# Moving the first-round transposes of an attention head pair past the next pair's first scores, in a decoder layer on one core

## The chip, the cores and the metric

The kernel runs on 1 core of one Trainium2 chip. The metric is the device time of one execution in microseconds (us), as the median of several runs. Engines are named as the profile names them: PE is TensorE (PEld its weight loads), DVE is VectorE, ACT is ScalarE, POOL is GpSimd, SP is SyncE.

## The reference

A pre-norm decoder layer on x (2 batches, 512 tokens, 128 channels): causal self-attention, differential cross-attention over 154 context tokens, and a quantised feed-forward with a depthwise convolution. Only the self-attention matters here:

```python
q = jnp.einsum('ntc,hdc->nhtd', x_q, w_q)          # 16 heads of 64
k = jnp.einsum('ntc,hdc->nhtd', x_q, w_k)
v = jnp.einsum('ntc,hdc->nhtd', x_q, w_v)
a = jnp.einsum('nhtd,nhsd->nhts', q, k) / math.sqrt(q.shape[3])
a = jnp.where(causal_forbidden[None, None], -jnp.inf, a)
a = jax.nn.softmax(a, axis=3)
y = jnp.einsum('nhts,nhsd->nthd', a, v).reshape(a.shape[0], t, -1)
return y @ w_o
```

## The kernel before

The self-attention is a software pipeline over 16 steps (STEPS: 2 batches of 8 head pairs). Step n treats both heads of one pair. Its 512 query rows are four tiles of 128 rows; because of the causal mask tile t has 128(t+1) key columns. They are taken in three rounds, `ROUNDS = [[3], [2, 0], [1]]`: round 0 is tile 3 (512 columns), round 1 tiles 2 and 0 (384 and 128), round 2 tile 1 (256), each for both heads. I call round 0 the first, round 1 the second and round 2 the short round.

A round passes through all engines. `scores(n, r)` on PE writes the scores to two PSUM banks; round k = 3n + r uses pair k % 2 of two such pairs (ST0 and its neighbour, SM and its neighbour), so scores(n, 2) must wait until the exponentials of round (n, 0) have read theirs (`exp_done`), and scores(n+1, 0) for those of round (n, 1). `row_max(n, r)` on DVE reduces them (L1122 for round 0, one instruction a head; L1128 for the others). `exps(n, r)` on ACT (L414) writes the exponentials and their sums. `invert_sums` on DVE (L1136) takes reciprocals, `normalise` on POOL (L299) multiplies with them. `turn(n, r)` on PE (L677) transposes the probabilities into PSUM, 64 by 64: rounds 0 and 1 into the same two banks PT and PT + 1 (16 transposes each), round 2 into PJ0 and OB (8 transposes). The turned blocks are copied to SBUF: `keep_turned(n, 0)` on DVE (128x512, L1150) and `keep_half(n)` on ACT (L423) share those of round 0, `keep_turned(n, 1)` on DVE copies those of round 1 (128x1024, also L1150), `keep_short(n)` on ACT those of round 2 (L435). Because rounds 0 and 1 share banks, turn(n, 1) waits until both copies of round 0 are done. `weighted(n)` on PE multiplies with the values, `copy_heads` on ACT (L445) takes the result.

`project(n+1, 1)` and `project(n+1, 0)` on PE make the keys and queries of the next pair. `keys(n+1)` on DVE (L1108) and `query(n+1)` on ACT (L393) copy them to `qs`. The query projection uses bank PT, so it waits for keep_turned(n-1, 1), and scores(n+1, 0) waits for query(n+1). On ACT `query(n+1)` stands behind `exps(n, 1)`.

Each engine works through its instructions strictly in the order written; the engines meet only through semaphores. `t_ps` counts finished turns, `pt_dve` and `pt_act` finished copies. Before the change the orders of step n are:

- PE: scores(n, 0), turn(n-1, 1), scores(n, 1), turn(n-1, 2), scores(n, 2), both projections of n+1, weighted(n-1), turn(n, 0).
- DVE: keep_turned(n-1, 0), row_max(n, 0), keep_turned(n-1, 1), invert_sums(n, 0), row_max(n, 1), row_max(n, 2), keys(n+1), extras of some steps, invert_sums(n, 1), invert_sums(n, 2), extras.
- ACT: copy_heads(n-2), keep_half(n-1), exps(n, 0), keep_short(n-1), exps(n, 1), query(n+1), exps(n, 2).

Some steps carry extras: DVE quantises the two feed-forward weights behind steps 2 and 3 (`quantise_weights`), takes norm statistics behind step 10 and applies the norm behind step 11; ACT takes a square root behind step 10, which swaps its function table twice; PE does the output projection of batch 0 in step 9 behind the projections (`out_proj`, waits for keys(10)) and four 128x128 transposes in step 12 (`turn_norm`, waits for keys(13)). After step 15 cross-attention rounds (`cross_max`, `cross_row_max`) follow, interleaved with the remaining turns of the last pair.

Of the kernel before, what the change touches and what calls it, by code (L numbers as in the profile page):

```python
# [18 lines left out]
STEPS = B * NPAIR  # L19
# [45 lines left out]
def decoder_layer(nc, x, consts, wqk, wv, wo, ctxT, xwq, xbq, xwk, xbk, xwv, xbv, xwo, xbo, lam_in,  # L65
                  w1, cw, cb, w2, out):
    with ExitStack() as ctx:
# [135 lines left out]
        def sem_names(*names):  # L203
            return [sem(n) for n in names]
# [10 lines left out]
        t_ps, pt_dve, pt_act, u_ps, u_done = sem_names("t_ps", "pt_dve", "pt_act", "u_ps", "u_done")  # L215
# [150 lines left out]
        def _(act):  # L366
# [38 lines left out]
            def exps(n, r):  # L405
                k = 3 * n + r
                if n >= 1:
                    act.wait_ge(t_ps, k - 2)
                at = 0
                for t in ROUNDS[r]:  # L410
                    w = P * (t + 1)
                    for a in range(2):
                        act.wait_ge(max_done, MAXES[k] + 1 + a if r == 0 else MAXES[k + 1])
                        nc.scalar.activation(prob[r][:, a, at:at + w], bank[:, SP[k % 2] + a, at:at + w], ACT.Exp,  # L414
                                             bias=nmax[:, t, a:a + 1], accum_out=psum[:, t, a:a + 1]).then_inc(exp_done, 1)
                    at += w
# [8 lines left out]

            def keep_short(n):

                act.wait_ge(t_ps, 3 * n + 3)
                if n >= 1:
                    act.wait_ge(u_ps, n)  # L430
                for half, at in enumerate((PJ0, OB)):
                    whole = pT[:, 2, :, :]
                    dst = bass.AP(whole.tensor, whole.offset + 64 * half,
                                  [list(whole.ap[0]), [T, 2], [P, 2], [1, 64]])
                    last = nc.scalar.copy(dst, bank[:, at, 0:2 * P].rearrange("p (a i q) -> p a i q", a=2, i=2))  # L435
                last.then_inc(pt_act, 1)
# [165 lines left out]
        def _(pe):  # L602
            def mm(out_, lhsT, rhs, start, stop, **kw):
                return nc.tensor.matmul(out_, lhsT, rhs, start=start, stop=stop, **kw)  # L604
# [21 lines left out]
            def scores(n, r):  # L626

                k = 3 * n + r
                if r == 0:
                    pe.wait_ge(q_done, n + 1)  # L630
                    pe.wait_ge(k_done, n + 1)
                if k >= 2:
                    pe.wait_ge(exp_done, EXPS[k - 1])
                at = 0
                for t in ROUNDS[r]:
                    w = P * (t + 1)
                    for a in range(2):
                        own = slice(64 * a, 64 * a + 64)
                        mm(bank[:, SP[k % 2] + a, at:at + w], qs[own, 0, t * P:t * P + P], qs[own, 1, 0:w], at == 0,
                           False, skip_group_check=True)  # L640
                    at += w
                    for half in range(2):
                        for a in range(2):
                            own = slice(64 * a, 64 * a + 64)
                            last = mm(bank[:, SP[k % 2] + a, at - P:at], sel_b[own, half, :], mask_b[own, half, :], False,
                                      half == 1, skip_group_check=True)
                last.then_inc(s_ps, 1)

            def turn(n, r):

                k, blocks = 3 * n + r, (NT, NT, 2)[r]
                pe.wait_ge(norm_done, EXPS[k + 1])
                if r == 0 and n >= 1:
                    pe.wait_ge(pt_dve, 2 * n)
                if r == 0 and n + 1 < STEPS:
                    pe.wait_ge(q_done, n + 2)
                if r == 1:
                    pe.wait_ge(pt_dve, 2 * n + 1)
                    pe.wait_ge(pt_act, 2 * n + 1)
                if r == 2:  # L660
                    if n + 1 < STEPS:
                        pe.wait_ge(k_done, n + 2)
                    else:
                        pe.wait_ge(xq_act, 2)
                    if n >= 1:
                        pe.wait_ge(u_done, n)
                    if n == 9:
                        pe.wait_ge(y_done, 1)
                    if n == 12:
                        pe.wait_ge(xTl_done, 3)  # L670
                lower, upper = (PJ0, OB) if r == 2 else (PT, PT + 1)
                for a in range(2):
                    for i in range(blocks):
                        at = 64 * (blocks * a + i)
                        for half, to in enumerate((lower, upper)):
                            own = slice(64 * half, 64 * half + 64)
                            last = nc.tensor.transpose(bank[:, to, at:at + 64], prob[r][own, a, P * i:P * i + P],  # L677
                                                       con[own, C_ID + 64 * half:C_ID + 64 * half + 64])
                last.then_inc(t_ps, 1)
# [54 lines left out]
            def next_round():  # L734
                r = rounds[0]
                rounds[0] += 1
                if r >= 1:

                    pe.wait_ge(round_done, r if r < SINGLE else r - 1)
                return _round_bank(r)  # L740
# [8 lines left out]
            def cross_max(G, r):  # L749
                b, g, t, half = G // NG, G % NG, r // 2, r % 2  # L750
                if r == 0:
                    pe.wait_ge(qb0_done, G + 1)
                    pe.wait_ge(km_done, 2 * G + 2)
                at = next_round()
                for k in range(2):
                    last = mm(bank[:, at + k, 0:2 * S2],
                              qb0[:, G % 2, t * P:t * P + P],
                              km[:, g, 4 * half + 2 * k:4 * half + 2 * k + 2, :], True, True)
                last.then_inc(round_ps, 1)
# [173 lines left out]
            project(1, 1)  # L933
            pe.wait_ge(wsum_done, 1)
            project(1, 0)
            turn(0, 0)
            pe.wait_ge(vx_done, 4)

            for n in range(1, STEPS):
                scores(n, 0)  # L940
                turn(n - 1, 1)
                scores(n, 1)
                turn(n - 1, 2)
                scores(n, 2)
                if n + 1 < STEPS:
                    project(n + 1, 1)
                    project(n + 1, 0)
                else:
                    pe.wait_ge(pt_act, 2 * STEPS - 2)
                    stack_queries(0)  # L950
                if n == 9:
                    for t in range(NT):
                        out_proj(0, t)
                if n == 12:
                    pe.wait_ge(k_done, 14)
                    turn_norm(0, 3, PJ0)
                weighted(n - 1)
                turn(n, 0)


            pe.wait_ge(exp_done, EXPS[3 * STEPS - 1])
            cross_max(0, 0)
            turn(STEPS - 1, 1)
            cross_max(0, 1)
            turn(STEPS - 1, 2)
            cross_max(0, 2)
            pe.wait_ge(pt_act, 2 * STEPS)
            stack_queries(1)
# [77 lines left out]
        def _(dve):  # L1046
# [91 lines left out]

            def keep_turned(n, r):

                dve.wait_ge(t_ps, 3 * n + r + 1)
                if r == 0 and n >= 2:
                    dve.wait_ge(u_ps, n - 1)
                if r == 1 and n >= 1:
                    dve.wait_ge(u_ps, n)
                slot = 1 if r else 3 * (n % 2)
                dst, src = turned_to(slot, 2 * NT), turned_from(PT, PT + 2, 2 * NT)
                if r == 0:
                    dst, src = dst[:, 0], src[:, 0]
                nc.vector.tensor_copy(dst, src).then_inc(pt_dve, 1)  # L1150
# [107 lines left out]
            link(nc.vector.memset(lam_c[:, 0:1], 1.0 - LAMBDA_INIT))  # L1258

            for n in range(1, STEPS):  # L1260
                keep_turned(n - 1, 0)
                row_max(n, 0)
                keep_turned(n - 1, 1)
                invert_sums(n, 0)
                row_max(n, 1)
                row_max(n, 2)
                if n + 1 < STEPS:
                    keys(n + 1)
                if n == 9:
                    residual(0, PJ0)  # L1270
                if n == 12:
                    turned_norm_low(0, 3, PJ0)
                invert_sums(n, 1)
                invert_sums(n, 2)
                if n in (2, 3):
                    quantise_weights(n - 2)
                if n == 10:
                    norm_stats(0)
                if n == 11:
                    norm_apply(0, 3)  # L1280
# [223 lines left out]
```

## Time and profile before

| What | Value |
|---|---|
| Median of 3 runs | 359.07 us (359.01 to 362.24) |
| Profiled execution, its own time | 358.9 us |
| Its span in the trace | 356.7 us |
| Busy, PE / DVE / ACT / POOL | 307.7 / 226.1 / 212.4 / 121.3 us |
| Step n = 1 of self-attention starts at | 43.36 us |
| Step n = 15 starts at | 178.69 us |

Here a step starts where PE starts scores(n, 0), the four matmuls of 64x512. A row of the timeline gives the start (us from the beginning of the span), the length of the group, engine, line, operation, what it writes and reads, how many instructions it merges, and in brackets how long its engine sat idle before it and which instruction released it. All matmuls carry L604 or L677, the lines of the helper and of the transposes, so they are told apart by their operands. Instructions that follow one another on DVE or ACT overlap in the trace by some 0.1 us, so the distance between two starts is the better length of a step of work.

### The profile page before, as it was taken

Reading aid. Unit: us, or ns where it says so; the run is one execution under the profiler, and the core shown is the slowest. Engines: PE = TensorE matmul, PEld = TensorE weight load, DVE = VectorE, ACT = ScalarE, POOL = GpSimd, SP = SyncE. Lnnn points to the kernel's source line nnn. Section 1 sums busy time; section 2 is a strip of 40 time slices with the busy share of each in tenths; the row PEclk is TensorE's granted clock in tenths of the full one; section 3 lists DMA queues with packets and bytes.
Section 4 is the critical chain, followed back from the end, with each engine's and each line's share of the span. In section 5 each row is a group of like instructions: output and inputs, shape, how many; then the busy total and the mean of one; then the engine's idle time right before and its main releaser. Section 6 shows DMA issues by size and latency. Waiting matters only on the chain.

```text
span 356.7 us, 6631 instructions
## 1 busy us (share of the span) xinstructions
PE 307.7 (86%) x2454; PEld 202.4 (57%) x2454; DVE 226.1 (63%) x507; ACT 212.4 (60%) x520; POOL 121.3 (34%) x193
## 2 busy tenths in 40 slices
PE   1797899989999998889997799969999897988795
PEld 0564665666666775656664467735655562465463
DVE  3854667776666527676666564576777768068554
ACT  3465577767777618867774173576786368436154
POOL 4623547774477646625642020113330000000000
PEclk9999899999999999999996889999999999999696
DMA  7800000000000000000000000000000000000001
GB/s 286 299 1 2 0 3 1 2 2 2 3 0 3 2 2 1 2 2 0 2 3 3 0 0 2 0 0 3 0 1 2 0 3 0 0 0 2 0 23 38
DMA packets 4834, 6.17 MB, mean 17 GB/s; under 512 B 833, under 2 KB 3649, under 8 KB 4674
## 3 DMA queue, kind: packets, MB, share of 16 engines
q1 hardware_dynamic: 4514, 5.42, 4.3%
q8 instruction: 19, 0.31, 0.4%
q10 hardware_dynamic: 288, 0.33, 0.3%
q14 instruction: 13, 0.11, 0.1%
HBM read 5.23 MB, written 0.52 MB: 16 GB/s over the span
## 4 chain that ended last, share of the span: by engine, by line
PE 57%; DVE 20%; ACT 14%; issue 6%; POOL 1%; DMA 1%; ACTq 0%; DVEq 0%
PE bank L604 51%; ACT pr L414 4%; ACT pT L414 3%; DVE nmax L1122 3%; DVE nmax L1128 3%; PE bank L677 2%; DVE pT L1150 2%; ACT pT L520 2%; PE bank L805 1%; DVE qk L1179 1%; DVE xn L1072 1%; ACT v_sb L525 1%; DVE onT L1302 1%; DVE stats L1059 1%; POOL pr L299 1%
## 5 line engine op out<-in xcount | busy, mean ns | idle before, releaser
L1179 DVE TENSOR_REDUCE qk<-bank 128x4 fp32r<-128x616 f32 x64 | 49.2, 797 | 24.6 <-PE bank L604 24.3
L520 ACT ACTIVATE pT<-bank 128x512 f32<-128x512 f32 (+1 forms) x80 | 45.0, 600 | 28.4 <-PE bank L604 27.3
L299 POOL TENSOR_SCALAR pr<-pr,pinv 128x384 f32<-128x384 f32 (+2 forms) x96 | 46.3, 505 | 45.1 <-DVE pinv L1136 45.1
L414 ACT ACTIVATE pr<-bank,nmax 128x384 f32<-128x384 f32 (+2 forms) x96 | 44.7, 482 | 18.2 <-DVE nmax L1128 18.2
L604 PE MATMUL bank<-qs 64*128 64x512 f32 (+3 forms) x256 | 49.0, 464 | 4.6 <-ACT pT L414 4.6
L604 PE MATMUL bank<-pT,v_sb 128*64 128x128 f32 (+2 forms) x320 | 39.5, 394 | 0.0
L309 POOL TENSOR_TENSOR km<-kb_,con 128x1232 fp32r<-128x1232 f32 x8 | 18.0, 2248 | 59.4 <-PE bank L604 57.4
L604 PE MATMUL bank<-km,qk 128*128 128x308 f32 x128 | 33.7, 347 | 3.9 <-ACT pr L414 2.0
L1150 DVE COPY pT<-bank 128x512 f32<-128x512 f32 (+1 forms) x32 | 30.4, 951 | 6.8 <-PE bank L677 6.7
L414 ACT ACTIVATE pT<-bank,nmax 128x512 f32<-128x512 f32 x32 | 21.7, 683 | 20.4 <-DVE nmax L1122 20.4
L604 PEld LDWEIGHTS bank<-pT,v_sb 128*64 128x64 f32 x320 | 21.8, 140 | 19.1 <-issue 16.9
L604 PEld LDWEIGHTS bank<-km,qk 128*128 128x128 f32 x128 | 23.8, 197 | 13.5 <-DVE qk L1179 5.0
L604 PE MATMUL bank<-qk,km 128*128 128x512 f32 x64 | 28.5, 451 | 2.3 <-ACT pT L520 2.0
L1128 DVE TENSOR_REDUCE nmax<-bank 128x2 f32<-128x768 f32 (+2 forms) x48 | 29.9, 676 | 0.6 <-PE bank L604 0.6
L299 POOL TENSOR_SCALAR pT<-pT,pinv 128x512 f32<-128x512 f32 x32 | 21.9, 697 | 21.4 <-DVE pinv L1136 21.4
L1136 DVE RECIPROCAL pinv<-psum 128x2 f32<-128x2 f32 x64 | 8.5, 157 | 29.0 <-ACT pr L414 28.1
L604 PEld LDWEIGHTS bank<-qs 64*128 64x128 f32 x256 | 20.2, 188 | 7.5 <-ACT pT L414 6.2
L1122 DVE TENSOR_REDUCE nmax<-bank 128x1 f32<-128x512 f32 x32 | 20.6, 683 | 4.2 <-PE bank L604 4.2
L604 PEld LDWEIGHTS bank<-mask_b,sel_b 64*128 64x128 bf16 x256 | 13.9, 94 | 16.3 <-issue 12.3
L677 PE MATMUL bank<-con,pr 64*128 64x64 f32 x384 | 18.4, 227 | 4.6 <-POOL pr L299 3.0
L414 ACT ACTIVATION_READ_ACCUMULATOR pr<-bank,nmax 128x1 f32 x96 | 20.5, 213 | 0.0
L604 PE MATMUL bank<-qk,wqk_h 128*128 128x512 f32 x48 | 19.2, 444 | 1.4 <-DVE wqk_l L1367 1.4
(162 smaller groups left out, 596.8 us busy)
## 6 DMA issues: line engine op xcount, KB each, us to landing
pT<-in_wqk SPq DMA_DIRECT2D x1, 1024.0 KB, 6.0
cw_sb<-in_cw SPq DMA_DIRECT2D x1, 768.0 KB, 8.9
x_sb<-in_x SPq DMA_DIRECT2D x2, 256.0 KB, 5.2
pT<-in_wv SPq DMA_DIRECT2D x1, 512.0 KB, 6.7
wo_sb<-in_wo SPq DMA_DIRECT2D x1, 512.0 KB, 7.2
out<-x_sb SPq DMA_DIRECT2D x8, 64.0 KB, 1.5
onT<-in_consts ACTq DMA_DIRECT2D x1, 256.0 KB, 6.5
pT<-in_xwk SPq DMA_DIRECT2D x1, 256.0 KB, 7.2
```

The costliest lines, as they stand in the source:

```text
L299: nc.gpsimd.tensor_scalar(d, d, pinv[:, t, a:a + 1], 1.0, ALU.mult, ALU.mult).then_inc(norm_done, 1)
L309: nc.gpsimd.tensor_tensor(km[:, g, :, :], _repeat(kb_[:, g, b, :], GP), _bcast(con[:, C_ROWM:C_ROWM + GP], S2), ALU.mult).then_inc(km_done, 1)
L414: nc.scalar.activation(prob[r][:, a, at:at + w], bank[:, SP[k % 2] + a, at:at + w], ACT.Exp, bias=nmax[:, t, a:a + 1], accum_out=psum[:, t ...
L520: nc.scalar.activation(px[rows, v % 10, :], bank[rows, (ST0, ST1)[v % 2], :], ACT.Exp, scale=SD ** -0.5).then_inc(xexp_done, 1)
L525: nc.scalar.copy(ut[:, G // NG, 2 * (G % NG) + u, :], bank[:, OB, :]).then_inc(ut_done, 1)
L604: return nc.tensor.matmul(out_, lhsT, rhs, start=start, stop=stop, **kw)
L677: last = nc.tensor.transpose(bank[:, to, at:at + 64], prob[r][own, a, P * i:P * i + P], con[own, C_ID + 64 * half:C_ID + 64 * half + 64])
L1122: nc.vector.tensor_reduce(nmax[:, NT - 1, a:a + 1], bank[:, SP[k % 2] + a, :], AX.X, ALU.max, negate=True).then_inc(max_done, 1)
L1128: last = nc.vector.tensor_reduce(nmax[:, t, :], bank[:, SP[k % 2]:SP[k % 2] + 2, at:at + w], AX.X, ALU.max, negate=True)
L1136: last = nc.vector.reciprocal(pinv[:, t, :], psum[:, t, :])
L1150: nc.vector.tensor_copy(dst, src).then_inc(pt_dve, 1)
L1179: nc.vector.tensor_reduce(m, s_in, AX.X, ALU.max, negate=True).then_inc(round_done, 1)
```

## The change

On PE turn(n-1, 0) leaves the end of step n-1 and goes between scores(n, 0) and scores(n, 1); turn(n-1, 1), which stood there, goes behind scores(n, 1) and behind turn(n-1, 2). On DVE row_max(n, 0) goes ahead of keep_turned(n-1, 0). The waits on `t_ps` are recounted for the new order 0, 2, 1: exps(n, 1) now waits for the third turn, keep_short for the second, keep_turned(n, 1) for the third. The end after step 15 is reordered in the same way. No arithmetic is added or removed.

```diff
--- before.py
+++ after.py
@@ -405,7 +405,7 @@
             def exps(n, r):
                 k = 3 * n + r
                 if n >= 1:
-                    act.wait_ge(t_ps, k - 2)
+                    act.wait_ge(t_ps, 3 * n - (2, 0, 1)[r])
                 at = 0
                 for t in ROUNDS[r]:
                     w = P * (t + 1)
@@ -425,7 +425,7 @@
 
             def keep_short(n):
 
-                act.wait_ge(t_ps, 3 * n + 3)
+                act.wait_ge(t_ps, 3 * n + 2)
                 if n >= 1:
                     act.wait_ge(u_ps, n)
                 for half, at in enumerate((PJ0, OB)):
@@ -933,14 +933,14 @@
             project(1, 1)
             pe.wait_ge(wsum_done, 1)
             project(1, 0)
-            turn(0, 0)
             pe.wait_ge(vx_done, 4)
 
             for n in range(1, STEPS):
                 scores(n, 0)
-                turn(n - 1, 1)
+                turn(n - 1, 0)
                 scores(n, 1)
                 turn(n - 1, 2)
+                turn(n - 1, 1)
                 scores(n, 2)
                 if n + 1 < STEPS:
                     project(n + 1, 1)
@@ -955,14 +955,14 @@
                     pe.wait_ge(k_done, 14)
                     turn_norm(0, 3, PJ0)
                 weighted(n - 1)
-                turn(n, 0)
 
 
             pe.wait_ge(exp_done, EXPS[3 * STEPS - 1])
+            turn(STEPS - 1, 0)
             cross_max(0, 0)
+            turn(STEPS - 1, 2)
             turn(STEPS - 1, 1)
             cross_max(0, 1)
-            turn(STEPS - 1, 2)
             cross_max(0, 2)
             pe.wait_ge(pt_act, 2 * STEPS)
             stack_queries(1)
@@ -1138,7 +1138,7 @@
 
             def keep_turned(n, r):
 
-                dve.wait_ge(t_ps, 3 * n + r + 1)
+                dve.wait_ge(t_ps, 3 * n + (3 if r else 1))
                 if r == 0 and n >= 2:
                     dve.wait_ge(u_ps, n - 1)
                 if r == 1 and n >= 1:
@@ -1258,8 +1258,8 @@
             link(nc.vector.memset(lam_c[:, 0:1], 1.0 - LAMBDA_INIT))
 
             for n in range(1, STEPS):
+                row_max(n, 0)
                 keep_turned(n - 1, 0)
-                row_max(n, 0)
                 keep_turned(n - 1, 1)
                 invert_sums(n, 0)
                 row_max(n, 1)
```

## Rows read from the trace of the kernel before

**Rows 1.** Windows of seven steps; columns: length, busy (count) per engine, PEclk, DMA share, GB/s.

```profile
52.09:60.81 8.72, 8.37 (x105) 5.57 (x102) 6.10 (x14) 6.43 (x22) 6.82 (x11) 1.00 0.00 1
60.81:70.59 9.78, 8.52 (x105) 5.63 (x102) 7.64 (x16) 6.60 (x22) 7.50 (x12) 1.00 0.01 2
70.59:80.06 9.47, 8.51 (x104) 5.63 (x102) 7.05 (x15) 6.60 (x22) 7.32 (x11) 1.00 0.01 2
88.77:97.76 8.99, 8.36 (x104) 5.56 (x102) 6.05 (x12) 6.48 (x22) 4.18 (x10) 1.00 0.01 3
115.19:131.62 16.43, 15.75 (x168) 12.78 (x166) 6.54 (x13) 6.50 (x22) 8.09 (x13) 1.00 0.00 1
140.33:150.96 10.63, 8.55 (x104) 5.65 (x102) 7.45 (x23) 9.13 (x25) 7.61 (x11) 1.00 0.01 2
150.96:161.28 10.32, 9.20 (x108) 6.04 (x106) 7.80 (x17) 7.08 (x23) 3.50 (x8) 1.00 0.01 2
```

**Rows 2.** Timeline of PE, step 2 (starts at 52.09).

```profile
53.12 0.69 PE L677 MATMUL bank<-con,pr 64*128 64x64 f32 x16
...
55.61 0.70 PE L604 MATMUL bank<-qs 64*128 64x256 f32 x4 [0.35 <-ACT pT L414]
...
57.94 2.38 PE L604 MATMUL bank<-pT,v_sb 128*64 128x384 f32 x20
60.26 0.72 PE L677 MATMUL bank<-con,pT 64*128 64x64 f32 x16
```

**Rows 3.** Timeline of DVE, step 2 and the begin of step 3.

```profile
53.33 1.29 DVE L1122 TENSOR_REDUCE nmax<-bank 128x1 f32<-128x512 f32 x2 [0.33 <-PE bank L604]
54.53 1.21 DVE L1150 COPY pT<-bank 128x1024 f32<-128x1024 f32 x1
...
55.73 1.86 DVE L1128 TENSOR_REDUCE nmax<-bank 128x2 f32<-128x768 f32 x3
57.52 0.68 DVE L1108 COPY qs<-bank 128x512 f32<-128x512 f32 x1
...
60.46 0.17 DVE L1136 RECIPROCAL pinv<-psum 128x2 f32<-128x2 f32 x1 [1.17 <-ACT pr L414]
...
62.38 0.69 DVE L1150 COPY pT<-bank 128x512 f32<-128x512 f32 x1
```

**Rows 4.** Timeline of ACT, step 2 and the begin of step 3.

```profile
54.11 0.69 ACT L414 ACTIVATE pT<-bank,nmax 128x512 f32<-128x512 f32 x1 [1.23 <-DVE nmax L1122]
...
57.09 0.58 ACT L414 ACTIVATE pr<-bank,nmax 128x384 f32<-128x384 f32 x1 [1.00 <-DVE nmax L1128]
...
58.91 0.61 ACT L393 ACTIVATE qs<-bank 128x512 f32<-128x512 f32 x1
...
61.02 0.59 ACT L423 COPY pT<-bank 128x512 f32<-128x512 f32 x1
```

**Rows 5.** Timeline of all engines just before step 1 (query copy, then transposes).

```profile
42.09 0.60 ACT L393 ACTIVATE qs<-bank 128x512 f32<-128x512 f32 x1 [2.49 <-PE bank L604]
...
42.84 0.72 PE L677 MATMUL bank<-con,pT 64*128 64x64 f32 x16 [0.78 <-ACT qs L393]
```

**Rows 6.** Timeline of POOL around the start of step 6 (at 88.77).

```profile
87.35 2.76 POOL L299 TENSOR_SCALAR pr<-pr,pinv 128x384 f32<-128x384 f32 x6 [2.11 <-DVE pinv L1136]
```

**Rows 7.** Timeline of DVE in step 4: the copy of round 0.

```profile
71.87 0.67 DVE L1150 COPY pT<-bank 128x512 f32<-128x512 f32 x1
```

**Rows 8.** Timeline of DVE in step 12: the copy of round 0.

```profile
152.32 0.68 DVE L1150 COPY pT<-bank 128x512 f32<-128x512 f32 x1
```

**Rows 9.** Timeline of PE: output projection in step 9, norm transposes in step 12.

```profile
121.44 7.38 PE L604 MATMUL bank<-wo_sb,onT 128*128 128x128 f32 x64 [0.33 <-DVE qs L1108]
...
157.83 0.65 PE L726 MATMUL bank<-con,xn 128*128 128x128 f32 x4 [0.17 <-DVE qs L1108]
```

**Rows 10.** Timeline of ACT: first exponential of the second round in steps 11 and 15.

```profile
147.19 0.58 ACT L414 ACTIVATE pr<-bank,nmax 128x384 f32<-128x384 f32 x1 [0.94 <-DVE nmax L1128]
...
183.97 0.58 ACT L414 ACTIVATE pr<-bank,nmax 128x384 f32<-128x384 f32 x1 [1.28 <-DVE nmax L1128]
```

## The prediction

> **What bounds the kernel now.** I read first the busy times by step, then the timeline of one step on each engine, then the steps that stand out. The change touches the 15 steps from 43.36 to 188.9 us; the rest keeps its code. In an ordinary step TensorE is busy 8.37 of 8.72 us, ScalarE 6.43, VectorE 6.10 [rows 1], and the granted clock is 1.00, its level of 2.4 GHz. Eight steps (1, 2, 5, 7, 8, 10, 13, 14) take 8.70 to 8.73 us, 69.7 together. Where is their one gap? Before scores(n, 2) TensorE sits idle 0.35 us until the last exponential of round 0 is done [rows 2]. The chain to it starts with scores(n, 0): the row maxima start 1.24 us after the step does (53.33 - 52.09, rows 1 and 3), the first exponential at 2.02, and scores(n, 2) 1.50 us behind that, at 3.52 [rows 2, 4]. From there TensorE does not stop until the next step. So the cycle is TensorE's work plus this gap. The gap is what moving work under it could fill; what the move puts behind one another is the question.
>
> **The change in an ordinary step.** Times are from the start of scores(n, 0), which I call 0. No instruction is added, removed or made longer, and no DMA is issued or passed.
>
> *Round 0.* Row maxima run from 1.24 to 2.44 (54.53 - 53.33 is 1.20 for both) [rows 3]. On TensorE turn(n-1, 0) starts behind the scores at 1.03 (53.12 - 52.09) [rows 2], its result is there at 1.03 + 0.72 = 1.75, and keep_half starts 0.04 later (61.02 against 60.26 + 0.72), ends at 2.4 [rows 2, 4]. It now stands ahead of exps(n, 0) on ScalarE with its work not yet done, so the first exponential goes from 2.02 to about 2.27 (copy of 0.59, less 0.1 overlap), and scores(n, 2) can't start before 3.77. Since the 0.55 us of turn 0 (60.81 - 60.26) left the end of the step, this alone would be a gain of 0.3 us a step.
>
> *Round 1.* Here is the loss. keep_turned(n-1, 0) on VectorE now stands behind the maxima: 2.44 to 3.13 (0.69 long) [rows 3]. turn(n-1, 1) needs its banks free; TensorE has by then issued turn 0, scores(n, 1) and the short turn, and is ready at some 3.1. A hand-over to TensorE costs up to 0.15 (42.09 + 0.60 = 42.69, then 42.84) [rows 5]: start at 3.28. Its transposes take 0.69 [rows 2], the hand-over back 0.04: the copy of 128x1024, keep_turned(n-1, 1), starts at 4.01. Before the change it started at 2.44 (54.53) and lay inside the wait for the exponentials. VectorE takes its work in order, so invert_sums(n, 0) and row_max(n, 1), whose scores have long been there, wait behind it. row_max(n, 1) comes 1.20 after the copy's start (55.73 - 54.53) [rows 3]: 5.21 instead of 3.64. exps(n, 1) comes 1.36 behind that (57.09 - 55.73): 6.57. query(n+1) stands behind exps(n, 1) on ScalarE, 1.82 later (58.91 - 57.09): 8.39, and takes 0.61 [rows 4]: 9.00. scores(n+1, 0) needs it, with 0.15 for the hand-over: **9.15**. Before the change the same copy ended at 7.43 (58.91 + 0.61 - 52.09), 1.3 us before it was needed. TensorE's own work would be done at 3.77 + 2.33 + 2.32 = 8.42 (scores(n, 2) and the projections 57.94 - 55.61 = 2.33, weighted 60.26 - 57.94 = 2.32) [rows 2], so it stands idle for 0.7 us there. The gap before scores(n, 2) goes, and a wait twice as long comes before scores(n+1, 0). An ordinary step goes from 8.71 to 9.15, and eight of them cost 8 x 9.15 - 69.7 = **+3.5**. Step 6, 8.99 before [rows 1]: **+0.2**.
>
> *GpSimd* is not late: its six normalisations of rounds 1 and 2 end at 90.11, 1.34 into the step [rows 6]; exps(n, 1) now ends 1.14 later against the next step's start ((9.15 - 6.57) = 2.58 ahead of it instead of 60.81 - 57.09 = 3.72), which gives 2.48, and the short turn needs them at about 2.75 (0.55 for turn 0 and some 1.2 for scores(n, 1) behind 1.03). Cover of 0.27; if it fails, that much is added.
>
> **Steps with extras.** The second invert_sums comes 1.55 behind query's start (60.46 - 58.91): at 9.94, which is 0.79 after the next step's start; before it was 0.35 ahead of it. What VectorE has behind it now pushes the row maxima too, which stood behind keep_turned(n-1, 0) before and now open the chain.
> - Step 3: 62.38 - 60.46 = 1.92 of work [rows 3], so the maxima start at 0.79 + 1.92 = 2.71 instead of 1.24: 9.15 + 1.47 = 10.6 against 9.78, **+0.8**.
> - Step 4: the copy starts 1.28 in [rows 1, 7], so 1.63 of work by the same 0.35: delay 1.18, 10.3 against 9.47, **+0.9**.
> - Step 12: 1.36 in [rows 1, 8], 1.71 of work, delay 1.26. Its norm transposes wait for keys(13), which start 1.79 behind row_max(12, 1) (57.52 - 55.73): 5.21 + 1.26 + 1.79 + 0.68 + 0.05 = 8.99; then 0.60 for them [rows 9] and 2.32 for weighted: 11.9 against 10.32, **+1.6**. TensorE is the last there, not the query.
> - Step 9: out_proj waits for keys(10): 5.21 + 1.79 + 0.68 + 0.15 = 7.83, then 7.38 [rows 9] and 2.32: 17.5 against 16.43, **+1.1**.
> - Step 11: the table swaps start 1.14 later against the step, so its exps(11, 1) starts at 147.19 - 140.33 + 1.14 = 8.00 instead of 6.57: 9.15 + 1.43 = 10.6 against 10.63 [rows 1, 10], **0**.
> - Start: turn(0, 0) no longer stands ahead of scores(1, 0); it took 0.52 (43.36 - 42.84) [rows 5]. A wait for a VectorE result remains: **-0.3**.
> - End: exps(15, 1) at 6.57 instead of 5.28 (183.97 - 178.69) [rows 10], and cross_max(0, 0) behind it: +1.3. Then turn 1 and its copy fall behind the short turn, between nothing and the copy's 1.2 us; I take 0.5, since the short turn waits for little. **+1.8**.
>
> Sum: 3.5 + 0.2 + 0.8 + 0.9 + 1.6 + 1.1 + 0 - 0.3 + 1.8 = **+9.6 us**, on the profiled execution's own 358.9: 368.5. The median is 0.17 above it, so 368.6, +2.7%. Behind step 15 nothing absorbs it: the chain there starts with this cross_max.
>
> **Bounds.** The order is certain, the hand-overs are not: rows show 0.04 to 0.15, which over the two to TensorE in the loop is up to 0.2 less a step, -3 us. 0.1 more (the overlap of two copies may be lost) is +1.4. The end may cost 1.3 less 0.5 or, with TensorE slower there, 2.5 more. That gives 365 to 373.
>
> **Rivals.**
> - *TensorE stays the bound* and the gap is filled. For it: it is busy 96% of the step. Against it: it would take a loop shorter by 0.73 us than the rows add up to, or a query that doesn't wait behind exps(n, 1). Each ordinary step then takes 8.42: 8 x 8.42 - 69.7 = -2.3, step 6 -0.6, the start -0.3, the others about nothing: 355.7, -0.9%. The Trainium skill ("Perfetto Trace Analysis", Identifying the Most-Contended Engine) says to find the engine with the highest occupancy and close the gaps on it; by that rule TensorE is the one, and this is its result. Faster than now the change becomes once the loop falls under 8.71, 0.44 less than my sum. 6%.
> - *The new chain is shorter by half of what it is over the old step*: 8.9 a step, +1.8 in all for ordinary ones, and steps with extras at half: near 362.5. 7%.
> - *The clock falls.* Now it holds 1.00 in every step, also in step 11 with 8.55 of 10.63 us busy [rows 1], which speaks against it within the loop. Behind step 15 TensorE waits for the exponentials 1.3 us longer than now; a drop to 1.2 GHz there would double what it covers, some 2.5 us and more: 371 to 375. 12%.
> - *My forecast*, new wait for the query copy: 368.6. 75%.
>
> The range is 364.5 to 373. A time within 1% (355.5 to 362.7) can't be told from no change in this kernel. Faster by over 1%: 0.03, within: 0.08, slower: 0.89.
>
> **What would show it.** In the trace after: scores(n, 0) of ordinary steps 9.1 to 9.2 us apart; TensorE idle about 0.7 us before it, released by the query copy, and no gap of 0.35 before scores(n, 2); a wait of 0.1 to 0.3 before turn(n-1, 1), released by the VectorE copy; VectorE idle some 0.9 us between its two copies; row_max(n, 1) at 5.2 in the step; ScalarE idle over 2 us before exps(n, 1). Steps 3, 4, 9 and 12 are the longest losers, step 11 none. The prediction is wrong if the query copy ends before TensorE is through with weighted, that is, before 8.4.

## The result and the profile after

The changed kernel takes 368.1 us (median of 4 runs, 367.4 to 368.5) against 359.0 of the kernel before: a ratio of 1.023, 95% interval 1.017 to 1.030. The forecast was 368.6. The profiled execution took 368.5 us, 9.6 more than that of before; its span is 366.6, 9.9 more. Single executions more than 1.5% above the fastest of their kernel are left out of every time and ratio below; there was one each in experiments 7 and 8.

The first lines of the page after give the span and, for each engine, busy time, share and number of instructions. TensorE had 307.7 before, VectorE 226.1, ScalarE 212.4: the work is nearly the same, the waits have grown.

```profile
span 366.6 us, 6632 instructions
...
PE 310.9 (85%) x2454; PEld 201.6 (55%) x2454; DVE 226.3 (62%) x507; ACT 210.2 (57%) x520; POOL 120.9 (33%) x193
```

The windows of six steps after, to be held against [rows 1]. Columns: length, busy (count) per engine, granted clock, DMA share, GB/s.

```profile
51.89:60.95 9.06, 8.58 (x98) 5.46 (x98) 5.96 (x12) 6.27 (x22) 6.81 (x11) 1.00 0.01 2
60.95:71.54 10.59, 8.78 (x99) 5.55 (x99) 7.56 (x16) 6.38 (x22) 7.37 (x11) 1.00 0.01 2
71.54:81.94 10.40, 8.78 (x99) 5.54 (x99) 7.44 (x15) 6.37 (x22) 7.30 (x11) 1.00 0.01 2
118.21:135.67 17.46, 15.80 (x162) 12.68 (x162) 6.71 (x14) 7.13 (x25) 8.76 (x14) 1.00 0.00 1
144.74:156.00 11.26, 8.77 (x98) 5.68 (x99) 7.42 (x21) 9.79 (x28) 8.27 (x11) 1.00 0.01 1
156.00:167.26 11.26, 9.11 (x105) 5.94 (x103) 8.26 (x19) 7.07 (x24) 3.48 (x8) 1.00 0.01 1
```

An ordinary step (1, 2, 5, 6, 7, 8, 10, 13, 14) takes 9.06 or 9.07 us, all nine alike. Its timeline on TensorE, step 2, which starts at 51.89, to be held against [rows 2]:

```profile
51.89 1.13 PE L604 MATMUL bank<-qs 64*128 64x512 f32 x4 [0.42 <-ACT qs L393]
...
55.67 0.69 PE L604 MATMUL bank<-qs 64*128 64x256 f32 x4
...
58.15 2.38 PE L604 MATMUL bank<-pT,v_sb 128*64 128x384 f32 x20
60.95 1.13 PE L604 MATMUL bank<-qs 64*128 64x512 f32 x4 [0.41 <-ACT qs L393]
```

The 0.35 us gap before scores(n, 2) is gone: 55.67 - 51.89 = 3.78, forecast 3.77. In its place TensorE waits 0.42 and 0.41 us before scores(n, 0), released by the query copy (L393); in steps from 8 on it is 0.48 or 0.49, where it is there. VectorE in the same step [rows 3]:

```profile
53.17 1.29 DVE L1122 TENSOR_REDUCE nmax<-bank 128x1 f32<-128x512 f32 x2 [0.23 <-PE bank L604]
54.37 0.68 DVE L1150 COPY pT<-bank 128x512 f32<-128x512 f32 x1
55.91 1.23 DVE L1150 COPY pT<-bank 128x1024 f32<-128x1024 f32 x1 [0.85 <-PE bank L677]
...
57.12 1.87 DVE L1128 TENSOR_REDUCE nmax<-bank 128x2 f32<-128x768 f32 x3
```

The row maxima of round 0 start at 1.28 in the step, the copy of round 0 at 2.48, then VectorE is idle 0.85 us for the transposes, the copy of 128x1024 starts at 4.02 and row_max(n, 1) at 5.23. The forecast had 1.24, 2.44, 4.01 and 5.21. ScalarE [rows 4]:

```profile
53.67 0.59 ACT L423 COPY pT<-bank 128x512 f32<-128x512 f32 x1 [0.45 <-PE bank L677]
54.15 0.69 ACT L414 ACTIVATE pT<-bank,nmax 128x512 f32<-128x512 f32 x1
...
58.48 0.58 ACT L414 ACTIVATE pr<-bank,nmax 128x384 f32<-128x384 f32 x1 [2.34 <-DVE nmax L1128]
...
60.29 0.61 ACT L393 ACTIVATE qs<-bank 128x512 f32<-128x512 f32 x1
```

keep_half (53.67) stands ahead of the first exponential and delays it to 2.26. ScalarE then has nothing to do for 2.34 us before exps(n, 1), at 6.59; the query copy starts at 8.40. The forecast had 2.27, 6.57 and 8.39. The query copy ends at 60.90, and scores(n+1, 0) starts at 60.95, 0.05 behind it.

Two of the signs that the prediction named came weaker than written. Steps are 9.06 to 9.07 us, not 9.1 to 9.2. And turn(n-1, 1) starts at 3.27 after a pause of 0.07 us, not 0.1 to 0.3, for which the profile names no releaser; in steps 3 and 4 the same pause is 1.16 and 1.03 us. GpSimd was not late in step 2: its normalisations ended at 54.45, 0.22 us before the short turn started.

### The profile page after: what moved, and what is told of

Same layout as the page of the kernel before. It is cut to its first block, busy times and chain, and to the rows that moved or that the text cites. A ratio compares the mean times of both kernels' runs of the same rounds, so it can differ in the third digit from the quotient of the medians.

```text
span 366.6 us, 6632 instructions
## 1 busy us (share of the span) xinstructions
PE 310.9 (85%) x2454; PEld 201.6 (55%) x2454; DVE 226.3 (62%) x507; ACT 210.2 (57%) x520; POOL 120.9 (33%) x193
## 3 DMA queue, kind: packets, MB, share of 16 engines
HBM read 5.23 MB, written 0.52 MB: 16 GB/s over the span
## 4 chain that ended last, share of the span: by engine, by line
PE 54%; DVE 20%; ACT 14%; issue 8%; POOL 2%; DMA 1%; ACTq 0%; DVEq 0%
PE bank L604 45%; ACT pr L414 6%; PE bank L677 6%; DVE nmax L1128 5%; DVE pT L1150 3%; POOL pr L299 2%; ACT pT L520 2%; PE bank L805 1%; DVE qk L1179 1%; ACT qs L393 1%; ACT v_sb L525 1%; DVE onT L1302 1%; DVE stats L1059 1%; DMA x_sb<-in_x 1%; DVE xn L1072 1%
## 5 line engine op out<-in xcount | busy, mean ns | idle before, releaser
L604 PEld LDWEIGHTS bank<-mask_b,sel_b 64*128 64x128 bf16 x256 | 13.0, 94 | 16.9 <-issue 12.6
```

## The experiments

All eight ran with the kernel before on the same chips; its median there was 360.3 (1 to 4) and 360.4 (5 to 8), so the ratios count. The changed kernel was not run again there: totals and ratios of the changed kernel and of 1, 3 and 4 overlap, and those four are told apart by their traces alone, one for each kernel. "Steps" is the distance between the starts of steps 1 and 15, "end" from there to the end of the span; the numbers of the last three columns come from the profiled execution.

| Kernel | Median us | Ratio to before | 95% interval | Ordinary step | Steps | End |
|---|---|---|---|---|---|---|
| before | 359.0 | 1 | | 8.71 | 135.3 | 178.0 |
| after | 368.1 | 1.023 | 1.017 to 1.030 | 9.07 | 142.6 | 181.2 |
| 1 turns in order 0, 1, 2 | 367.8 | 1.021 | 1.015 to 1.027 | 9.07 | 142.7 | 180.9 |
| 2 row_max(n, 1) first | 354.8 | 0.986 | 0.981 to 0.991 | 8.75 to 8.83 | 133.1 | 177.2 |
| 3 query first | 367.6 | 1.021 | 1.015 to 1.026 | 8.86 to 8.93 | 141.5 | 181.1 |
| 4 TensorE moves only | 366.9 | 1.018 | 1.014 to 1.023 | 9.32 | 143.2 | 179.1 |
| 5 after, with a dose | 373.9 | 1.040 | 1.035 to 1.046 | 9.40 | 147.8 | 181.4 |
| 6 before, with a dose | 361.8 | 1.005 | 1.002 to 1.008 | 8.73 | 137.3 | 179.5 |
| 7 as 2, end reordered | 354.7 | 0.985 | 0.980 to 0.989 | 8.75 to 8.84 | 133.1 | 177.3 |
| 8 before, row_max(n, 1) first | 364.2 | 1.011 | 1.007 to 1.014 | 9.18 to 9.28 | 139.7 | 178.9 |

**The dose (5 and 6).** A maximum nobody uses is put ahead of row_max(n, 1), in the changed kernel and in the one before (the new tile `spare` is declared elsewhere):

```diff
                 invert_sums(n, 0)
+                dve.wait_ge(s_ps, 3 * n + 2)
+                link(nc.vector.tensor_reduce(spare[:, :], bank[:, SP[(3 * n + 1) % 2]:SP[(3 * n + 1) % 2] + 2, 0:P], AX.X, ALU.max))
                 row_max(n, 1)
```

> The changed kernel plus one short maximum on VectorE (two heads of 128 columns, result unused) ahead of row_max(n, 1), some 0.33 us of VectorE a step; nothing is left out. Theory (row_max(n, 1) lies on the loop that sets the step): every ordinary step grows by the whole dose, 9.07 to about 9.40; in all +4.5 to +5.5 us, 372.5 to 373.5. Rival (TensorE's work sets the step and the wait before scores(n+1, 0) only shares it): less than half of the dose, 370 or less.

> The kernel before plus the same 0.33 us maximum at the same place. Theory: there the query copy was done 1.3 us before it was needed, so the dose is absorbed; at most 0.1 us a step comes through keep_half, which ends some 0.2 us before turn 1 needs it: ordinary step 8.71 to 8.85, in all 0 to +1.5 us. Rival (VectorE's maxima are on the path in the kernel before too, and the change only added to it): +0.33 a step, +4.5 us in all.

In the changed kernel the ordinary step grew by the whole dose, 9.07 to 9.40, and so did TensorE's wait for the query copy, from 0.41 to 0.76 us. TensorE, start of step 3 of the dosed changed kernel (the added line moves the numbering by one):

```profile
61.75 1.13 PE L605 MATMUL bank<-qs 64*128 64x512 f32 x4 [0.76 <-ACT qs L394]
```

The total rose by 5.8 us, a little more than expected. Step 11 took 12.81 us, 1.55 more than in the changed kernel, and this is not the dose alone: TensorE's granted clock, 1.00 in all other steps, fell there, and the 4.65 us of work behind scores(n, 2) took 6.19. Step 12 gave 0.27 back.

```profile
148.20:161.01 12.81, 10.30 (x98) 6.55 (x98) 8.47 (x25) 10.02 (x28) 9.54 (x14) 0.87 0.01 1
```

In the kernel before, the same instruction cost 0 to 0.03 us an ordinary step. Its TensorE timeline in step 2 still has the old gap and the old releaser, even 0.05 shorter:

```profile
56.48 0.70 PE L605 MATMUL bank<-qs 64*128 64x256 f32 x4 [0.30 <-ACT pT L415]
```

That tells the two theories apart: row_max(n, 1) is on the path that sets the step after the change and was not before it. The 2.0 us that the steps of the dosed kernel before did lose lie in steps 3, 4, 9, 11 and 12 (0.3, 0.3, 0.3, 0.3 and 0.6), where VectorE has extra work or TensorE waits for the key copy: there VectorE was the path already.

**Row maximum ahead of the copy (2).** One move on VectorE in the changed kernel:

```diff
-                keep_turned(n - 1, 1)
-                invert_sums(n, 0)
                 row_max(n, 1)
+                keep_turned(n - 1, 1)
+                invert_sums(n, 0)
```

> The changed kernel with one move on VectorE: row_max(n, 1) ahead of the copy keep_turned(n-1, 1); nothing else. Theory (that copy in front of row_max(n, 1) is what lengthens the loop): exps(n, 1) starts 4.4 to 4.8 us into the step instead of 6.5, the query copy is no longer late, the copy runs at 4.3 to 5.5 and holds the query projection by 0.2 us: ordinary step 8.6 to 8.75, TensorE not waiting before scores(n+1, 0). In all -5 to -6 us against the changed kernel: 362 to 363, still a little over the kernel before because of the steps with extras and the end. Rival (the wait comes from elsewhere: keep_half ahead of exps(n, 0), or the transposes later): the step stays near 9.07, 367 to 368. Other rival: the late copy is now the bound, since both projections and the value product stand behind it: over 8.9.

The mechanism came as expected, the gain was more than twice as large, and the ordinary step came out up to 0.08 us over the range written. Step 2 starts at 51.45 in this kernel. VectorE: row_max(n, 1) at 3.08 in the step, the copy behind it at 4.28.

```profile
54.53 1.28 DVE L1128 TENSOR_REDUCE nmax<-bank 128x2 f32<-128x768 f32 x2
55.73 1.22 DVE L1150 COPY pT<-bank 128x1024 f32<-128x1024 f32 x1
```

ScalarE: exps(n, 1) at 4.46 instead of 6.59, the query copy at 6.62, now behind the projection and no longer behind the exponentials.

```profile
55.91 0.58 ACT L414 ACTIVATE pr<-bank,nmax 128x384 f32<-128x384 f32 x1 [0.21 <-DVE nmax L1128]
...
58.07 0.60 ACT L393 ACTIVATE qs<-bank 128x512 f32<-128x512 f32 x1 [0.23 <-PE bank L604]
```

TensorE: a wait of 0.16 us for the copy before the query projection is all that is left, and scores(n+1, 0) follows weighted without a gap.

```profile
57.09 0.47 PE L604 MATMUL bank<-xT_h,wqk_h 128*128 128x512 f32 x1 [0.16 <-DVE pT L1150]
...
60.28 1.13 PE L604 MATMUL bank<-qs 64*128 64x512 f32 x4
```

The step is 8.83 and, from step 7 on, 8.75: a little over the 8.71 of before. What I had missed is that everything behind row_max(n, 1) comes earlier too: the last reciprocal of step 2 starts 0.67 us ahead of step 3 (59.61 against 60.28), where it was 0.89 behind its start in the changed kernel (61.84 against 60.95):

```profile
59.61 0.17 DVE L1136 RECIPROCAL pinv<-psum 128x2 f32<-128x2 f32 x1 [1.27 <-ACT pr L414]
```

```profile
61.84 0.17 DVE L1136 RECIPROCAL pinv<-psum 128x2 f32<-128x2 f32 x1 [1.17 <-ACT pr L414]
```

So VectorE's extras hardly reach the row maxima any more: step 3 takes 9.10 (9.78 before, 10.59 after), step 4 8.82 (9.47, 10.40), step 11 9.84 (10.63, 11.26), step 12 9.71 (10.32, 11.26), and the end 0.8 us less than before. I had left those terms as they were in the changed kernel. Against the changed kernel the steps gave 9.5 us and the end 4.0; of the 4.0 some 1.1 is TensorE's clock, which fell later here: the 24 transposes after step 15 took 0.96 instead of 1.54 us and the product with the values 3.51 instead of 4.08. This version beats both kernels.

**Is the change needed for that gain? (8)** The same move made in the kernel before:

> The kernel before with only the VectorE move of the second experiment: row_max(n, 1) ahead of keep_turned(n-1, 1); the orders of TensorE and all else as before the change. It tells whether the 5 us gained there need the change at all. Theory A (they need it: before the change scores(n, 1) ends only at 2.75 us, so row_max(n, 1) waits for it, the copy behind it ends at 5.3 and holds the query projection by 0.4 us while the 0.35 us gap before scores(n, 2) stays): ordinary step 9.0 to 9.1; steps 3, 4, 11 and 12 gain some 0.5 each: 360 to 363. Theory B (the VectorE move alone does it): ordinary step 8.7 or less, 353 to 356.

It is needed: alone the move loses 1.1%, and with the change it gains 1.4% over the kernel before. TensorE in step 8, which starts at 108.71; the row at 104.95 belongs to step 7:

```profile
104.95 0.50 PE L604 MATMUL bank<-xT_h,wqk_h 128*128 128x512 f32 x1 [0.20 <-DVE pT L1150]
...
112.23 0.70 PE L604 MATMUL bank<-qs 64*128 64x256 f32 x4 [0.35 <-ACT pT L414]
```

Both waits are there: 0.35 us before scores(n, 2), since nothing was moved under it, and one for the copy before the query projection, which starts at 5.43 in the step instead of 5.07. The ordinary step is 9.2, 0.1 over the upper end that I gave, and the total 364.2, 1.2 over it. Steps 4, 11 and 12 came to 9.47, 10.02 and 10.58: only step 11 gained, where I had expected all four with extras to.

**Query ahead of the exponentials (3).** On ScalarE, in the changed kernel:

```diff
+                if n + 1 < STEPS:
+                    query(n + 1)
                 exps(n, 1)
-                if n + 1 < STEPS:
-                    query(n + 1)
-                else:
+                if n + 1 == STEPS:
                     query_parts(0)
```

> The changed kernel with one move on ScalarE: query(n+1) ahead of exps(n, 1). Theory (scores(n+1, 0) waits for the query copy only because that stands behind exps(n, 1)): the query copy runs at 6.4 to 7.0, exps(n, 1) from 7.0 to 8.8, and scores(n+1, 0) now waits for exps(n, 1), whose banks it needs: ordinary step 8.85 to 8.95, TensorE's wait before it now released by exponentials. In all -1.5 to -2.5 us: 365.5 to 366.5. Rival (the query copy is only the last name on a wait that the product with the values sets): no change, 9.07 and 368.

The wait before scores changed its releaser as the theory says (start of step 15):

```profile
184.60 1.13 PE L604 MATMUL bank<-qs 64*128 64x512 f32 x4 [0.28 <-ACT pr L414]
```

The step fell to 8.93 and 8.87, inside what I had written, so the query copy was a link of the loop. The total moved only 0.5 us, less than I expected: steps 11 and 12 rose by 0.3 and 0.6 (11.56 and 11.85) and step 1 started 0.3 later. The last is scatter, for the edit touches nothing ahead of step 1: in the four kernels with the same code there (changed, 3, 4 and 5) it starts at 42.82, 43.14, 42.55 and 42.96. Why steps 11 and 12 rose was not followed; the clock stayed at 1.00 in both. By the total alone this run can't be told from the rival; by the releaser and the step length it can.

**Moves on TensorE only (4).** VectorE's order as before the change:

```diff
-                row_max(n, 0)
                 keep_turned(n - 1, 0)
+                row_max(n, 0)
                 keep_turned(n - 1, 1)
```

> The changed kernel with the VectorE part undone: keep_turned(n-1, 0) ahead of row_max(n, 0) again, so only the moves on TensorE are left. Theory: the copy waits for turn 0 at 1.8, the row maxima of round 0 start at 2.4 instead of 1.2, exps(n, 0) at 3.2, scores(n, 2) at 4.7 instead of 3.8, and TensorE's work behind it (4.65 us) then ends at 9.35: TensorE's gap before scores(n, 2) comes back at 0.9 us and sets the step, 9.3 to 9.4, not the query copy. In all +3 to +4 us against the changed kernel: 371 to 372. Rival (the loop over the query copy sets the step whatever stands ahead; here it is 0.1 us shorter since the copy of round 0 comes earlier): 8.9 to 9.0, 366 to 367.

In the ordinary step the theory holds: 9.32, and the old gap is back at 0.97 us (step 15, starts at 185.74), with the exponentials as releaser:

```profile
190.41 0.70 PE L604 MATMUL bank<-qs 64*128 64x256 f32 x4 [0.97 <-ACT pT L414]
```

But the total was 366.9, below the changed kernel, not 3.5 us over it. Steps 3, 4 and 12 are those of the kernel before (9.80, 9.44, 10.36), because the copy of round 0, which waits for transposes until 1.8 in the step anyway, again stands between the extras and the maxima; and the end is 2.1 us shorter than in the changed kernel. So the change's VectorE move gains 0.25 us in each of eight ordinary steps and 0.5 in step 6, and gives more than that back in steps 3, 4, 9 and 12 (0.8, 1.0, 0.3 and 0.9).

Step 11 took 12.28 here against 11.26, but that is TensorE's clock and not work added by the order. After a pause of 2.00 us before scores(n, 2) the granted clock fell, and from there to the next step it took 6.16 us instead of 4.65:

```profile
144.47:156.75 12.28, 10.26 (x100) 6.50 (x98) 8.14 (x24) 9.48 (x26) 9.05 (x13) 0.86 0.01 1
...
150.59 0.85 PE L604 MATMUL bank<-qs 64*128 64x256 f32 x4 [2.00 <-ACT pT L414]
```

At the upper level the step would have been 6.12 + 4.65 = 10.77 us, an estimate from these rows, and thus shorter than in the changed kernel. In the end, too, the clock counts. Of the 2.1 us, 0.28 are there at cross_max(0, 0), which came at 11.49 in step 15. The 24 transposes behind it then took 1.03 us here and 1.54 in the changed kernel, the product with the values 3.32 and 4.08, in the same order of instructions; the granted clock from 197 to 200 was 0.80 here and 0.56 there.

```profile
198.03 1.03 PE L677 MATMUL bank<-con,pr 64*128 64x64 f32 x24 [0.25 <-POOL pr L299]
...
203.68 3.32 PE L604 MATMUL bank<-pT,v_sb 128*64 128x384 f32 x20
```

That is some 1.3 us more, in all 1.6 of the 2.1; the rest was not followed. What sets the clock apart here, where TensorE was busy 1.07 of the 3 us from 194 to 197 against 0.71 there, was not tested.

**Turn 1 ahead of the short turn (1).**

```diff
                 scores(n, 1)
-                turn(n - 1, 2)
                 turn(n - 1, 1)
+                turn(n - 1, 2)
                 scores(n, 2)
```

(with the three waits on t_ps counted for that order, and the same at the end)

> The changed kernel with one part of the change undone: turn(n-1, 1) stands ahead of the short turn again (both still behind scores(n, 1)), and the waits are counted for that order; the same at the end behind step 15. Theory (the step is set by the loop copy of round 0, turn 1, its copy, row_max(n, 1), exps(n, 1), query copy): turn 1 can't start before the copy of round 0 is out, 3.3 us into the step, in either order, so an ordinary step stays at 9.07 us and TensorE still waits 0.4 us for the query copy; at the end turn 1 comes some 0.5 us earlier. In all 0 to -1.5 us against the changed kernel: 366.8 to 368.3. Rival (putting the short turn first delays turn 1 and is the cost): the step falls by the 0.28 us of the short turn to 8.8, in all -4 us: 364.

Step and total did not move, as expected; the picture inside did, which I had not foreseen. keep_short stands behind the short turn, so the key projection now waits for it (0.23 us), and TensorE is without a gap before scores(n+1, 0). TensorE, step 2, starting at 51.94:

```profile
55.20 0.97 PE L677 MATMUL bank<-con,pr 64*128 64x64 f32 x24 [0.33 <-issue]
...
57.00 0.47 PE L604 MATMUL bank<-xT_h,wqk_h 128*128 128x512 f32 x1 [0.23 <-ACT pT L435]
```

The wait of 0.33 us before turn 1 is the one for the copy of round 0 (in the changed kernel it is hidden inside a merged row of 24 transposes, at 3.27). Two paths are 9.07 us long in this variant. Step 3 took 11.99 and step 4 9.07, together as in the changed kernel, but not for the same reason: in step 3 TensorE's granted clock fell after a pause of 1.86 us before turn 1, and a projection matmul took 0.63 instead of 0.40 us. Step 4 then began so late that VectorE's extras no longer reached its row maxima, which started at 1.28 in the step as in an ordinary one.

```profile
61.00:72.99 11.99, 9.90 (x98) 6.37 (x98) 8.07 (x18) 7.34 (x25) 8.76 (x14) 0.86 0.01 2
...
65.80 0.96 PE L677 MATMUL bank<-con,pr 64*128 64x64 f32 x24 [1.86 <-issue]
...
68.16 0.63 PE L604 MATMUL bank<-xT_h,wqk_l 128*128 128x512 f32 x1
```

The run refutes that the short turn's 0.28 us in front of turn 1 is the cost; it doesn't show which of the two paths holds the step.

**The end (7).** Version 2 with the second cross row maximum ahead of the last copy:

```diff
             cross_row_max(0, 0)
+            cross_row_max(0, 1)
             keep_turned(STEPS - 1, 1)
-            for r in range(1, 8):
+            for r in range(2, 8):
```

> The kernel of the second experiment (row_max(n, 1) first) with one more move on VectorE, behind step 15: the second cross row maximum goes ahead of the last copy of 128x1024, which only the last product with the values needs. Theory: cross_max(0, 2) waits there for that maximum, which waits for the copy (it starts 3.8 us behind cross_max(0, 0)); it comes 1.1 us earlier and the product with the values, still later than the copy, follows: -0.5 to -1.2 us, 353.7 to 354.3. Rival (the stretch is set by TensorE at its lower clock and by the later maxima): no change, 354.8, or the gap moves to the product: +0.

cross_max(0, 2) came 3.14 us behind cross_max(0, 0) instead of 3.79, but the four transposes that close the stretch came 13.03 instead of 13.11 behind it. The end is 177.3 against 177.2: no gain in the trace. The totals can't tell: 354.7 against 354.8, and single executions lie between 353.4 and 356.3. The wait moved to cross_max(0, 3), whose maximum now stands behind the copy, and the product with the values took 3.83 us instead of 3.51.

## Why the prediction was right, point by point

- **Ordinary step.** The loop copy of round 0, turn 1, its copy, row_max(n, 1), exps(n, 1), query, scores was right to 0.04 us at each station up to the query copy. The one term clearly off is the last hand-over, 0.05 instead of 0.15 us: 9.07, not 9.15. Eight of these steps cost +2.8 (72.5 - 69.7), forecast +3.5. TensorE's own work ended at 8.65, not 8.42, so its wait was 0.41 to 0.49, not 0.7. Of the 0.23 that its work came later, 0.15 lies in the projections, about half of it before the query projection, which starts 0.14 behind the end of the 128x1024 copy, and the rest mostly behind the product with the values.
- **Extras.** Step 3 +0.8 (forecast +0.8), step 4 +0.9 (+0.9), step 9 +1.0 (+1.1). Steps 11 and 12 together were right, 22.52 against 22.5 us, one by one they were not: +0.6 instead of 0 and +0.9 instead of +1.6. In step 11 TensorE, not the query copy, was last: scores(n, 2) waited 1.42 us for the exponentials behind the table load and started at 151.35, 6.61 in the step; with the 4.65 us that follow it that is 11.26. The forecast had taken the loop's value alone. The shift carried into step 12, where the norm transposes started at 8.35 instead of 8.99:

```profile
151.35 0.70 PE L604 MATMUL bank<-qs 64*128 64x256 f32 x4 [1.42 <-ACT pT L414]
...
164.35 0.65 PE L726 MATMUL bank<-con,xn 128*128 128x128 f32 x4 [1.48 <-DVE qs L1108]
```

- **Start.** -0.5 instead of -0.3: scores(1, 0) began at 42.82.
- **End.** The term most mis-sized: +3.2 instead of +1.8. TensorE in the kernel before, then in the changed one (cross_max(0, 0), cross_max(0, 2) and the product with the values):

```profile
188.92 0.52 PE L604 MATMUL bank<-km,qk 128*128 128x308 f32 x2 [2.05 <-ACT pr L414]
...
192.26 0.88 PE L604 MATMUL bank<-km,qk 128*128 128x308 f32 x2 [0.72 <-DVE qk L1179]
...
194.87 3.69 PE L604 MATMUL bank<-pT,v_sb 128*64 128x384 f32 x20
```

```profile
197.16 0.72 PE L604 MATMUL bank<-km,qk 128*128 128x308 f32 x2 [2.20 <-DVE qk L1169]
...
201.53 0.88 PE L604 MATMUL bank<-km,qk 128*128 128x308 f32 x2 [1.23 <-DVE qk L1179]
...
204.14 4.08 PE L604 MATMUL bank<-pT,v_sb 128*64 128x384 f32 x20
```

cross_max(0, 0) came 11.77 into the step instead of 10.23 (+1.5, forecast +1.3). cross_max(0, 2) came 4.37 us behind it instead of 3.34 (+1.0, forecast +0.5). Experiment 1, with turn 1 first, has 4.06 there. Experiment 4, with the same order of instructions in this stretch and the clock falling later, has 3.85, so about 0.5 of the +1.0 is the clock. The 20 matmuls of the product took 4.08 instead of 3.69 us, 0.4 more by the clock. The windows of the changed kernel show TensorE at its lower level, 1.2 GHz, there:

```profile
197.00:200.00 3.00, 2.76 (x28) 2.18 (x28) 1.96 (x4) 0.87 (x3) 0.98 (x4) 0.56 0.00 0
...
203.00:206.00 3.00, 3.00 (x14) 1.59 (x14) 1.05 (x2) 1.26 (x2) 0.00 (x0) 0.50 0.02 5
```

It fell after TensorE had been busy 0.71 us of the 3 from 194 to 197. In the kernel before it fell there too, which the prediction had not seen: TensorE was busy 1.00 of 3 us from 187 to 190, and the granted clock was 0.62 from 190 to 193 and 0.50 behind that. So what the change adds is an earlier fall, some 0.9 us of the +3.2, an estimate from the two differences above. The rival of the falling clock had 2.5 us there, and its total of 371 to 375 did not come. In the steps of the changed kernel the clock stayed at 1.00, as the prediction argued, but the margin is thin: it fell inside the loop in experiments 1 (step 3), 4 and 5 (step 11), for 1.4 to 1.5 us each time. In step 11 experiment 5 had the same three last pauses as the changed kernel, 0.52, 0.56 and 1.42 us, and the clock fell in the one and held in the other. What decides it stays open.

- **The other rivals and the total.** TensorE as the bound with its gap filled did not come true in the change. In experiment 2 TensorE has hardly a gap left, but its step takes 8.75 to 8.83 us, not that rival's 8.42: the sum of TensorE's own work was too low there too. Nor was the new chain half as long over the old step as forecast: the step grew by 0.35 of the 0.44. The misses upward (end +1.4, step 11 +0.6) and downward (ordinary steps -0.7, step 12 -0.7, start -0.2) cancel to 0.3 us: that the total came so close is luck.

## What to carry to other kernels

Before a gap on the busiest engine is filled, add up what the move puts behind one another in the orders of the other engines: here transposes moved some 2 us later held back a copy on VectorE, and the next pair's row maximum stood behind that copy. In this kernel it helped to move the row maximum too, ahead of the copy that now waits; with that one more move +2.3% became -1.4%, while the same move alone cost 1.1%. A dose of a third of a microsecond at one place, in both kernels, tells in two runs whether that place is on the path. And before the length of a step is put down to an order, its granted clock has to be read: one step at 0.86 hid the sign of a difference here.

## What the runs showed that I had not expected

The hand-over from a ScalarE copy to a waiting matmul was 0.05 us in the changed kernel (60.90 to 60.95), while the one in [rows 5] shows 0.15. And an order that makes the ordinary step longer can still make the kernel shorter: experiment 2 has steps of 8.75 to 8.83 against 8.71 and is 1.4% faster, since steps 3, 4, 11 and 12, those with extra work, are together 2.7 us shorter. The least expected was that TensorE's clock can fall in a step after a pause of 1.86 or 2.00 us, or after pauses with which it held in another kernel.
